# Graph layers of a one-core kernel: edge bodies without loops, two steps to a sum, one-hots made six at a time

## The reference

```
for l in range(4):                                # L0_gnn, four relations
    h   = einsum('ni,rio->rno', X, W[l])
    msg = h[etype, src] * inv_deg[:, None]
    out = segment_sum(msg, dst) + X @ root[l] + bias[l]
    X   = elu(layernorm(out) * gamma + beta) + X
...
all_h = einsum('ni,rio->nro', xn, weight)         # L1_gnn, eight relations
agg   = segment_sum(all_h[src, rel], dst)         # no weights on the edges
```

## Time and profile before

| what | us |
|---|---|
| median of three executions without the profiler | 8136.87 (8130.45 to 8153.14) |
| span of the profiled execution, first to last instruction | 10023.0 |
| busy in it: PE, DVE, ACT, POOL | 5916.0, 4244.2, 2864.4, 4208.7 |
| granted TensorE clock, mean | 0.763 |

### The profile page before, as it was taken

How to read it: one execution, slowest core, us unless ns; L and a number is a source line. 1 busy time by engine, 2 the same in 40 slices (tenths; PEclk the granted TensorE clock), 3 DMA queues, 4 the chain that set the end, 5 groups by cost and what they waited for, 6 DMA issues and landing times. The chain is left out here.

```text
span 10023.0 us, 108434 instructions
## 1 busy us (share of the span) xinstructions
PE 5916.0 (59%) x17886; PEld 3613.9 (36%) x17886; DVE 4244.2 (42%) x14584; ACT 2864.4 (29%) x8012; POOL 4208.7 (42%) x4288
## 2 busy tenths in 40 slices
PE   0676666656666666666654455486684444444368
PEld 0333333333443433344432222254343333333245
DVE  6134444444555545555544444423434333333422
ACT  0233333333333334444422222221122222221122
POOL 0045555545555545555555555400004444442311
PEclk9887778777777778888866666698796666667689
DMA  1433333333333333333332222200242222221000
GB/s 58 152 112 100 94 96 98 95 106 104 102 102 105 105 103 106 103 104 101 105 112 77 80 80 78 76 0 0 94 133 71 65 69 63 64 65 35 1 18 18
DMA packets 479373, 814.03 MB, mean 81 GB/s; under 512 B 88659, under 2 KB 343207, under 8 KB 478715
## 3 DMA queue, kind: packets, MB, share of 16 engines
q0 software_dynamic: 200480, 548.02, 19.4%
q1 hardware_dynamic: 278488, 262.51, 7.9%
HBM read 614.04 MB, written 196.16 MB: 81 GB/s over the span
## 5 line engine op out<-in xcount | busy, mean ns | idle before, releaser
L537 POOL DMA_INDIRECT gnn_msg<-tables,gnn_row_ring x4165 | 3986.1, 957 | 3934.9 <-ACT gnn_meta_ring L503 2309.4
L585 PE MATMUL bank<-gnn_msg,gnn_hot 128*128 128x256 f32 x8330 | 3200.0, 509 | 2783.6 <-DVE sums L566 1650.7
L585 PEld LDWEIGHTS bank<-gnn_msg,gnn_hot 128*128 128x128 f32 x8330 | 1810.5, 243 | 4141.7 <-DVE sums L566 2324.7
L566 DVE TENSOR_TENSOR sums<-sums,bank 128x256 f32 x4165 | 1744.7, 419 | 3103.8 <-issue 1507.2
L701 PE MATMUL bank<-gnn_w,residual 128*128 128x512 f32 x1176 | 644.6, 632 | 37.1 <-DVE sums L669 27.1
L527 ACT ACTIVATE gnn_hot<-gnn_away,gnn_meta_ring 128x128 f32<-128x128 f32 x1568 | 646.1, 483 | 50.0 <-remote 3.4
L515 ACT ACTIVATE gnn_away<-iota,gnn_meta_ring 128x128 f32<-128x128 f32 x1960 | 625.9, 391 | 29.4 <-DMA residual<-in_L_mix_b_dram 13.6
L546 DVE TENSOR_SCALAR gnn_hot<-iota,gnn_meta_ring 128x128 f32<-128x128 f32 x1764 | 615.7, 349 | 15.1 <-issue 8.5
L134 POOL TENSOR_TENSOR ve<-mv,eps 128x7 f32<-128x7 f32 x35 | 7.1, 204 | 1354.2 <-DVE mv L128 1206.1
L675 ACT ACTIVATE gnn_own<-gnn_own 128x256 f32<-128x256 f32 x196 | 81.6, 416 | 1351.8 <-DVE gnn_own L655 1339.0
L502 ACT COPY gnn_row_ring<-row 128x9 int32 (+1 forms) x490 | 94.1, 192 | 1057.3 <-PE bank L585 688.8
(11 more groups left out here) (392 smaller groups left out, 6690.7 us busy)
## 6 DMA issues: line engine op xcount, KB each, us to landing
tables<-residual SPq DMA_DIRECT2D x294, 256.0 KB
gnn_msg<-tables,gnn_row_ring POOLq DMA_INDIRECT x4165
tables<-sums SPq DMA_DIRECT2D x98, 512.0 KB, 2.9
tables<-gnn_msg SPq DMA_DIRECT2D x98, 256.0 KB, 2.1
residual<-first_norm_columns SPq DMA_DIRECT2D x98, 128.0 KB
first_norm<-state SPq DMA_DIRECT2D x1, 6272.0 KB, 22.5
first_rows<-residual SPq DMA_DIRECT2D x1, 6272.0 KB, 39.1
residual<-first_norm SPq DMA_DIRECT2D x49, 128.0 KB
```

The costliest lines, as they stand in the source:

```text
L537: self.nc.gpsimd.indirect_dma_start(out=self.msg[:, s0 + u, :], out_offset=None, in_=table, in_offset=bass.IndirectOffsetOnAxis(ap=self.ro ...
L566: self.nc.vector.tensor_tensor(at, at, self.sums(s, phase), ALU.add).then_inc(self.added, 1)
L585: self.nc.tensor.matmul(self.sums(s, phase), self.hot[:, s, :], self.msg[:, s, :], start=True, stop=True).then_inc(self.summed, 1)
```

## The change

- The loops are gone: all 49 bodies of each pass are written out, on all engines, so that waits have constants for targets and sources have fixed addresses. Only the address in `agg` still comes from a register.
- A body has 18 steps, and two neighbouring steps (`JOIN`) belong to the same tile and are summed by two matmuls into one PSUM bank. VectorE adds 9 times a body (`SUMS`), and the steps of a tile are rounded up to an even count. A pass has 882 steps.
- `body_row` has 10 entries for a body; two sets of registers take turns, and the load for the next body stands in VectorE's queue behind the add of sum 6.
- The ring copies are gone: gathers and one-hots read `c.row4` and `c.meta` where they lie. A gather's slot is free when the sum of the body before that read it is done; GpSimd waits for that itself, at every second gather.
- ScalarE makes no one-hots. VectorE makes them six at a time (`PARTS`): a TENSOR_TENSOR of 128 x 768 that compares the iota row with the places (both spread by broadcast), and in the first four passes a second one in place that multiplies by the weights. They are made for the next body, as soon as the six slots are free.

```diff
-SLOTS = 17
-HALVES = ((0, 9), (9, 8))
+JOIN = 2
+SLOTS = 18
+SUMS = SLOTS // JOIN
+PARTS = ((0, 6), (6, 6), (12, 6))
+TILES_AT = SUMS - 3
-AT_ONCE = 4
...
-                then(v.tensor_scalar(cnt_i[:], cnt[:], float(P - 1), None, ALU.add))
-                then(v.tensor_scalar(cnt_i[:], cnt_i[:], 7, None, ALU.arith_shift_right))
-                then(v.tensor_copy(nst[:], cnt_i[:]))
+                then(v.tensor_scalar(cnt_i[:], cnt[:], float(JOIN * P - 1), None, ALU.add))
+                then(v.tensor_scalar(cnt_i[:], cnt_i[:], (JOIN * P).bit_length() - 1, None, ALU.arith_shift_right))
+                then(v.tensor_scalar(nst[:], cnt_i[:], float(JOIN), None, ALU.mult))
...
-    def ring(self, act, i, n, h):
...
-    def scalar_hots(self, act, n, h):
...
     def gpsimd(self, pool, n, table):
-        for h, (s0, w) in enumerate(HALVES):
-            pool.wait_ge(self.ring_ready, n * 4 + (2 * h + 2))
-            gate(pool, self.c)
-            for u in range(w):
-                self.nc.gpsimd.indirect_dma_start(
-                    out=self.msg[:, s0 + u, :], out_offset=None, in_=table,
-                    in_offset=bass.IndirectOffsetOnAxis(ap=self.row_ring[:, h, u:u + 1], axis=0)).then_inc(self.landed[s0 + u], 16)
+        for s in range(SLOTS):
+            if n and s % JOIN == 0:
+                pool.wait_ge(self.summed, (n - 1) * SUMS + s // JOIN + 1)
+            at = n % NT * SLOTS + s
+            self.nc.gpsimd.indirect_dma_start(
+                out=self.msg[:, s, :], out_offset=None, in_=table,
+                in_offset=bass.IndirectOffsetOnAxis(ap=self.rows[:, at:at + 1], axis=0)).then_inc(self.landed[s], 16)
...
+    def begin_hots(self, dve, n, k):
+        s0, w = PARTS[k]
+        at = n % NT * SLOTS + s0
+        if n:
+            dve.wait_ge(self.summed, (n - 1) * SUMS + -(-(s0 + w) // JOIN))
+        self.nc.vector.tensor_tensor(self.hot[:, s0:s0 + w, :], self.c.iota[:].unsqueeze(1).to_broadcast([P, w, P]),
+                                     self.c.local[:, at:at + w].unsqueeze(2).to_broadcast([P, w, P]), ALU.is_equal)\
+            .then_inc(self.hot_begun if self.weighted else self.hot_ready, 1)
+
+    def end_hots(self, dve, n, k):
+        if not self.weighted:
+            return
...
+        dve.wait_ge(self.hot_begun, n * len(PARTS) + k + 1)
+        self.nc.vector.tensor_tensor(to, to, self.c.weight[:, at:at + w].unsqueeze(2).to_broadcast([P, w, P]), ALU.mult)\
+            .then_inc(self.hot_ready, 1)
...
+    def vector(self, dve, n, after, last=False):
+        tiles = self.tiles
+        for p in range(SUMS):
+            dve.wait_ge(self.summed, n * SUMS + p + 1)
+            if n or p:
+                dve.wait_ge(self.added, n * SUMS + p)
+            at = self.c.agg[:, ds(tiles[p] * D, D)]
+            self.nc.vector.tensor_tensor(at, at, self.sums(n, p), ALU.add).then_inc(self.added, 1)
+            if not last:
+                for k, (s0, w) in enumerate(PARTS):
+                    if (s0 + w - 1) // JOIN == p:
+                        self.begin_hots(dve, n + 1, k)
+            for s in range(p * JOIN, (p + 1) * JOIN):
+                after(s)
+            if not last:
+                if p == TILES_AT:
+                    self.tiles = body_tiles(dve, self.c, n + 1)
+                for k, (s0, w) in enumerate(PARTS):
+                    if (s0 + w - 1) // JOIN == p:
+                        self.end_hots(dve, n + 1, k)
+
+    def tensor(self, pe, n, after):
         for s in range(SLOTS):
+            p = s // JOIN
+            for k, (s0, w) in enumerate(PARTS):
+                if s == s0:
+                    pe.wait_ge(self.hot_ready, n * len(PARTS) + k + 1)
+            if s % JOIN == 0 and n * SUMS + p >= SUM_SLOTS:
+                pe.wait_ge(self.added, n * SUMS + p - SUM_SLOTS + 1)
             pe.wait_ge(self.landed[s], n * 16 + 16)
...
+            ins = self.nc.tensor.matmul(self.sums(n, p), self.hot[:, s, :], self.msg[:, s, :],
+                                        start=(s % JOIN == 0), stop=(s % JOIN == JOIN - 1))
+            if s % JOIN == JOIN - 1:
+                ins.then_inc(self.summed, 1)
             after(s)
-
-
-def each_body(eng, first, last, body):
...
```

More of the change, by code:

```diff
@@ L575, in tensor @@
-    def tensor(self, pe, n, phase, after):
-        for s in range(SLOTS):
-            pe.wait_ge(self.landed[s], n * 16 + 16)
-            h = 0 if s < HALF else 1
-            u = s - HALVES[h][0]
-            if u < DVE_HOTS[h]:
-                pe.wait_ge(self.hot_ready, n * sum(DVE_HOTS) + (h * DVE_HOTS[0] + u + 1))
-            else:
-                pe.wait_ge(self.act_hot_ready, n * 2 * ACT_HOTS + (h * ACT_HOTS + u - DVE_HOTS[h] + 1))
-            pe.wait_ge(self.added, n * SLOTS + (SLOTS + s - SUM_SLOTS + 1))
-            self.nc.tensor.matmul(self.sums(s, phase), self.hot[:, s, :], self.msg[:, s, :], start=True, stop=True).then_inc(self.summed, 1)
-            after(s)
@@ L589, in each_body, with use @@
-def each_body(eng, first, last, body):
-    n = (last - first) // AT_ONCE
-    for i in range(first, last - n * AT_ONCE):
-        body(i, i)
-    first = last - n * AT_ONCE
-    with eng.Fori(0, n) as g:
-        for j in range(AT_ONCE):
-            body(g * AT_ONCE + (first + j), first + j)
+        self.hot_begun, self.hot_ready, self.summed, self.added = (
+            c.sem(n) for n in ("hot_begun", "hot_made", "steps_summed", "steps_added"))
+        self.tiles = None
+    def use(self, msg, hot, rows, weighted):
+        self.msg, self.hot, self.rows, self.weighted = msg, hot, rows, weighted
@@ L1144, in gnn0 @@
         edges = c.edges = EdgeSum(nc, c)
-        edges.use(msg, hot, away, row_ring, meta_ring, c.row4, True)
+        edges.use(msg, hot, c.row4, True)
         post = Post(nc, c, ph, cutter(own), scratch, vecs, w)
@@ L1205, in _ @@
                     work.load(sp, 1)
-                    with sp.Fori(1, NT - 1) as i:
+                    for i in range(1, NT - 1):
                         t = ranked_tile(sp, c, i - 1)
@@ L1283, in _ @@
                     pe.sem_inc(s_tabs, 1)
-                def last_body(i, phase):
-                    edges.tensor(pe, i + LASTL * NT, phase + LASTL * NT, nothing)
-                each_body(pe, 0, NT, last_body)
+                for i in range(NT):
+                    edges.tensor(pe, i + LASTL * NT, nothing)
             @block.scalar
@@ L1335, in _ @@
                     act.wait_ge(kept, NG * 32 + 32)
-                act.wait_ge(s_root, NT)
-                for h in range(2):
-                    edges.ring(act, 0, 0, h)
-                edges.scalar_hots(act, 0, 0)
                 act.wait_ge(s_keep, 32)
@@ L1342, in _ @@
                     work.begin_scalar(act)
[L1343 removed]
                     work.scalar(act, 0, True, False)
[L1345 to L1349 removed]
+                    for i in range(1, NT):
                         n = i + l * NT
```

222 lines of the change are left out of this document (52 added, 170 removed).

## The result

The changed kernel takes 8372.7 us (median of four executions, 8365.36 to 8375.41), the kernel before on the same chip 8145.01. The ratio is 1.0278, with a 95% interval of 1.0259 to 1.0297: slower by 228 us. Forecast were 8570 us and slower; the measured time lies in the likeliest case's own range, 197 us under its centre.

What follows compares the result with a forecast made beforehand. The prediction took GpSimd's gathers to bound the kernel: 8137 + 306 for more gathers - 356 for removed waits + 481 for contention = 8568, say 8570 us. The range over all cases was 7910 to 8860 us.

Steps and rivals of the forecast that it cites:

- likeliest case: Whole kernel: wide one-hots hold up gathers by the worked-out amount, 8570 us, own range 8300 to 8850, chance 0.56.
- Which engine is the bound: Passes over the edges: GpSimd's gathers at 1.25 us each bound the timed kernel before, to within 5%.
- Gathers, +306 us: Edge passes: 4410 gathers in place of 4165, 245 more at 1.25 us each, add 306 us.
- I take all of it: Edge passes: dropping ring copies and loops removes all 356 us above gathers and outside time; other bound, nothing removed.
- Contention, +481 us: Edge passes: VectorE's wide one-hots with two SBUF inputs hold up gathers, adding 481 us; bounds nothing to 1260 us.
- the first rival: Edge passes: gathers and wide one-hots locked in phase so they miss each other, 8087 us, up to 8150; chance 0.12.
- Outside the passes, 2574.6 us: Everything but the five edge passes: no gather runs there and the change leaves its 2574.6 us nearly alone.
- The reading of the earlier trace: Gathers beside VectorE: two SBUF inputs hold a gather reading its row numbers 0.13 us in; one PSUM input costs nothing.
- The signs: Profile after: mean gather 1.05 to 1.1 us in passes 1 to 4, passes about 1210 and 1155 us.
- A shorter gather on the device: Gathers: half of the 0.30 us gap is the recorder's, so 1.10 us each and 7911 us; chance 0.20.
- TensorE as the bound: Edge passes: at 1.2 GHz TensorE's 18 steps take 22.0 us plus hook products, giving 8676 us; chance 0.09.
- Held for whole instructions: Edge passes: each wide one-hot shuts GpSimd out for its full 0.954 us, giving 9347 us; chance 0.03.

Runs made afterwards that it cites:

- unrolled: Kernel before with its edge bodies written out instead of looped, nothing else changed: 7980.5 us, ratio 0.9796.
- single17_narrow: Changed kernel with 17 steps of one sum each and one-hots made one at a time with one SBUF input: 7940.0 us, ratio 0.9748.
- single17_spread: Changed kernel with 17 single-sum steps and one-SBUF-input one-hots, one made after each sum instead of five or six in a row: 7827.6 us, ratio 0.9614.
- threes: Changed kernel with one-hots made three at a time instead of six, in 128x384 instructions: 8232.1 us, ratio 1.0102.
- dose_two: Changed kernel plus one unused 128x768 VectorE compare with two SBUF inputs per part of six one-hots: 8651.5 us, ratio 1.0615.
- iota_psum: Changed kernel with three PSUM banks for sums and the wide compares' iota operand in the fourth: 8206.4 us, ratio 1.0077.
- narrow: Changed kernel with one-hots made one at a time by a compare-and-multiply reading one SBUF tile, no wide multiply: 8142.5 us, ratio 0.9997.
- dose_one: Changed kernel plus one unused 128x768 VectorE compare with one SBUF tile and a per-partition scalar per part: 8482.4 us, ratio 1.0414.

## Why the prediction was right, step by step

**Which engine is the bound: right.** It hung on the conclusion that the recording slows VectorE and not GpSimd. Two kernels, `unrolled` and the changed one, show half of it: without loops the span equals the device's time, and gathers still come every 1.25 us, so the recording does not stretch them. That in the loops it is VectorE that the recording holds up rests on the earlier trace rows alone, and what in the loops does it was not tried.

**Gathers, +306 us: right in the changed kernel**, where the period is 1.251 us throughout. As the worth of the edit by itself it depends on the company: +337 with wide, +202 with narrow one-hots.

**"I take all of it", -356 us: right as a sum.** In the changed kernel nothing but lengthened gathers stands above the floor of its passes. But it has two parts that the prediction did not part: 162 us were the loops, and some 200 stayed in `unrolled`. Of these 56 are gathers lengthened by VectorE's instructions (the changed kernel has 12 beside those under its wide ones); the rest are waits for late sums and copies. 18 steps with 9 sums cover such waits (0.5 us of them are left in the changed kernel). 17 sums with one-hots in a row do not (103 in `single17_narrow`), spread ones nearly do (15 in `single17_spread`).

**Contention, +481 us: the mechanism right, the size wrong.** This is the term of the sum that was mis-sized: 330 us by the count, 316.6 of it under the wide instructions. The forecast had 0.364 us for each wide instruction: a chance of 0.76, times 0.48 us. It let an instruction hold every gather whose 0.13 us point it covers. The step that failed is this one: only an instruction that began some 0.04 us or more before the gather's start holds it. That takes 0.17 us off the 0.954, at the end where most is left to wait for. With phases spread evenly as before, the chance becomes 0.78 / 1.25 = 0.63 and the mean hold 0.39 us, so 0.25 us for each and 325 us for 1323 of them, where 316.6 were measured. The same working for the 0.55 us of `threes` gives 0.058 us (0.051 measured), for `dose_two` 0.25 (0.249). Measured for the two kinds were 188.9 / 735 = 0.257 for a compare and 127.7 / 588 = 0.217 for a multiply. 520 of 735 compares held a gather, for 0.36 us each, but only 234 of 588 multiplies, for 0.54. There the phases are partly locked, as the first rival had it (176 of those 234 gathers started 0.25 to 0.30 us after the multiply had begun), but not so as to miss always, and it moves the sum little. Taking the wide instructions away gave 230 us on the clock, since 50 us of lengthening remain, 18 us of waits came up and the pauses between passes grew.

**Outside the passes, 2574.6 us: 45 too much.** Measured are 2529.5. The pauses between the first four passes were taken from the recorded execution of before, where they were up to 37 us; they are 25 to 27, which is 27 us in all. The stretch after the last gather is another 19 us shorter. 45 and 151 us make 196 of the 199 by which the sum of 8568 missed the profiled 8369.0.

**The reading of the earlier trace rows: right in what it concluded, not in why.** L669 was taken to show that an instruction with one input from PSUM holds no gather. But it began 0.01 us after the gather's start, where two SBUF inputs hold none either. The row could not tell; `iota_psum` does. That "missing needs luck six times a body" leaned on the same oversight: 0.3 of the compares and 0.6 of the multiplies held no gather, where it counted on 0.24.

**The signs.** The mean gather was forecast at 1.05 to 1.1 us in passes 1 to 4 and is 1.02 to 1.03; passes 1210 and 1155 us, and are 1169 to 1175 and 1152. The rule that one is late "by what is left of it less 0.13 us" holds to 0.01 us in 741 of 743 cases where VectorE had begun at least 0.05 us before, and fails in all 142 where it had not by 0.03; the gather at 2403.36 is one of these. The forecast's own range has a slip: 8300 to 8850 is called a third to one and a half times of the 481 us, which from 8087 would be 8247 to 8809.

**The rivals.** No contention: excluded by the trace of after; the kernel that has nearly none, `narrow`, came out at 8142 where 8087 was worked out. A shorter gather on the device: excluded, 1.25 us stands in a span equal to the device's time. TensorE as the bound: within the passes GpSimd never waited over its usual pause, so no. But the argument against it, that the clock had no reason to fall lower than 0.76, was wrong: it was 0.55 in the fourth pass, with TensorE busy for 988 of 1173 us. It cost nothing here, in the pass with the fewest TensorE instructions of the five (1759 against 2533 to 3111). Held for whole instructions: never. The longest hold under a wide instruction was 0.79 us of its 0.954, and no wide instruction waited for a gather to end (1.03 us at most). The Trainium skill ("SBUF — State Buffer", Who interferes with whom) has the one that issues first keep the shared ports for its whole instruction, and the other blocked. The trace agrees on the order, and for VectorE's instructions on the length; a gather that came first held VectorE up for 0.08 us at most, not for its 0.946.

## What to carry to other kernels

Where GpSimd's gathers set the pace, count VectorE's instructions by where their operands lie: the long ones with two SBUF tensors, or with one in the fast mode, each hold a gather that starts 0.05 us or more after them until they end, while the same compare with one operand in PSUM is free. If they can't be avoided, make them short (0.051 us lost for one of 0.55 us, 0.239 for one of 0.955), and spread them between the instructions that others wait for. A row in which VectorE begins at the same moment as the gather says nothing on what holds it. And before believing the waits in a profile, compare its span with the timed execution; where they differ, a variant without loops tells which waits are real.

## What the runs showed of the hardware that was not expected

- A one-input `TENSOR_SCALAR` of 128 x 768 f32 takes 613 ns where a `TENSOR_TENSOR` of that size takes 955, and holds a gather too (0.108 us for each, against 0.249).
- What decides is who came first: in the changed kernel, gathers that started less than 0.03 us after a wide two-input instruction began, or before it, were not held (142, 0.3 us together), those that started 0.05 us or more after were (743 of 743).
- It goes the other way too. In `narrow`, the 706 weighted one-hots that began 0.40 to 0.65 us after a gather's start last 0.454 us on average, the other 2822 last 0.341. The 613 ns instruction of `dose_one` was not longer there (201 cases, 0.614 us). Why is not known.
- A `TENSOR_TENSOR` of 128 x 768 with one operand in PSUM is no slower (951 ns against 954) and held none of 541 gathers.
- In the kernel with loops the recorded execution was 1886 us longer than the timed one; with the same work written out, in 91308 recorded instructions in place of 108434, the difference was 3 us.
- The third pass ran at a mean granted clock of 0.88 to 0.95 and the fourth at 0.52 to 0.62 in the twelve profiles after that of before, and the fourth took at most 9 us more than the third (in the two dose kernels), and up to 161 us less (in `unrolled`).
